# Waits in another order, epsilon on VectorE, a shorter normalise on GpSimd, and a new order of all pieces in a hybrid attention kernel

## The reference

```
x = x + window_attention(layernorm(x))      # 16 heads of 8, 2 key/value heads, windows of 32, keys 64 wide
x = x + butterfly_ffn(layernorm(x))         # 128 -> 512, gelu, 512 -> 128
x = x + linear_attention(layernorm(x))      # phi(x) = elu(x) + 1, phi(q) (phi(k)^T v) / (phi(q) sum phi(k) + 1e-6)
x = x + butterfly_ffn(layernorm(x))         # the same weights again
layernorm(x) = (x - mean) / sqrt(var + 1e-5)
```

## Time and profile before

| | us |
|---|---|
| median of 3 runs | 561.26 (560.38 to 562.34) |
| profiled execution, span from first to last instruction | 560.6 |
| TensorE busy | 525.0 |
| GpSimd busy | 450.9 |
| VectorE busy | 441.2 |
| ScalarE busy | 358.7 |
| instructions | 14708, of them 5060 matmuls |
| bytes moved | 38.88 MB, mean 69 GB/s |

### The profile page before, as it was taken

The page is one execution under the profiler, slowest core; times in us unless marked ns, Lnnn a source line. Parts: engine busy times, 40 slices in busy tenths (PEclk is TensorE's granted clock), DMA queues, the critical chain, the costliest instruction groups (busy, mean ns, idle before and its releaser), DMA issues. The chain is left out here.

```text
span 560.6 us, 14708 instructions
## 1 busy us (share of the span) xinstructions
PE 525.0 (94%) x5060; PEld 345.8 (62%) x5060; DVE 441.2 (79%) x1272; ACT 358.7 (64%) x578; POOL 450.9 (80%) x646
## 2 busy tenths in 40 slices
PE   5786998979999999999999999999999999999795
PEld 3442554546766666666667676666666667777563
DVE  5778789897888989898988898888989797663341
ACT  2543376567687767676777768686767777664532
POOL 6665689899898999999898989899999797955420
PEclk9789799989999999999999999999999999999899
DMA  9533232322223232232313231323232222100001
GB/s 310 170 76 81 63 83 54 81 74 56 54 58 80 62 76 66 68 78 48 102 45 87 63 87 44 84 60 77 61 76 50 59 66 58 39 1 20 1 20 37
DMA packets 49546, 38.88 MB, mean 69 GB/s; under 512 B 12352, under 2 KB 38976, under 8 KB 49472
## 3 DMA queue, kind: packets, MB, share of 16 engines
q1 hardware_dynamic: 47024, 33.73, 23.9%
q10 hardware_dynamic: 2448, 4.22, 2.1%
HBM read 15.64 MB, written 5.51 MB: 38 GB/s over the span
## 5 line engine op out<-in xcount | busy, mean ns | idle before, releaser
L501 POOL TENSOR_TENSOR probs_t<-probs_t,first 128x1024 f32<-128x1024 f32 x64 | 151.3, 2367 | 11.5 <-DMA probs_t<-probs_t 11.5
L645 PEld LDWEIGHTS ring<-w,early 128*128 128x128 f32 x1024 | 119.0, 192 | 9.6 <-issue 7.0
L982 ACT ACTIVATE early<-ring,b 128x512 f32<-128x512 f32 x128 | 87.2, 684 | 54.7 <-PE ring L633 53.1
L645 PE MATMUL ring<-w,early 128*128 128x128 f32 x1024 | 120.0, 275 | 0.8 <-ACT early L982 0.8
L972 ACT ACT_TABLE_LOAD x58 | 74.4, 1283 | 10.7 <-issue 9.7
L601 PE MATMUL ps_s<-kx,q_t 64*32 64x512 f32 x960 | 65.9, 606 | 3.4 <-DVE merged L1268 2.7
L633 PE MATMUL ring<-xT_G,w1b 128*128 128x512 f32 x128 | 67.1, 612 | 0.7 <-ACT xT_G L960 0.7
L991 ACT ACTIVATE probs_t<-merged_t 128x1024 f32<-128x1024 f32 x64 | 65.3, 1044 | 3.8 <-DVE merged_t L1275 3.7
L633 PE MATMUL ring<-xT_F,w1b 128*128 128x512 f32 x128 | 59.9, 611 | 0.4 <-ACT xT_F L960 0.4
L1255 DVE COPY_PREDICATED ps_s<-first,ps_s 128x512 f32<-128x512 uint32 x64 | 43.6, 681 | 9.2 <-PE ps_s L601 9.0
L1282 DVE STREAM_TRANSPOSE ps_o<-ps_o 128x512 f32<-128x512 f32 x64 | 46.2, 722 | 1.6 <-PE ps_o L618 0.3
(11 more groups left out here) (124 smaller groups left out, 1023.9 us busy)
## 6 DMA issues: line engine op xcount, KB each, us to landing
probs_t<-probs_t SPq DMA_DIRECT2D x256, 64.0 KB, 2.0
kx<-kv_rows SPq DMA_DIRECT2D x120, 40.0 KB, 2.2
x_P<-in_x SPq DMA_DIRECT2D x16, 256.0 KB, 3.2
out_x<-x_G SPq DMA_DIRECT2D x16, 256.0 KB, 2.4
vx_t<-kv_rows SPq DMA_DIRECT2D x128, 8.0 KB
up_s<-in_up_m ACTq DMA_DIRECT2D x7, 256.0 KB, 8.4
down_s<-in_down_m ACTq DMA_DIRECT2D x7, 256.0 KB, 8.4
kv_rows<-kv_t SPq DMA_DIRECT2D x16, 80.0 KB, 2.8
```

The costliest lines, as they stand in the source:

```text
L501: nc.gpsimd.tensor_tensor(parts, parts, keep.rearrange("p (a t) -> p a t", a=1).to_broadcast([P, PAIR * HEADS, WIN]), ALU.mult).then_inc(p ...
L645: last = nc.tensor.matmul(bank(name)[:, P * j:P * (j + 1)], hid[s][:, c, P * j:P * (j + 1)], w2[:, c], start=(c == 0), stop=(c == CH - 1))
L982: nc.scalar.activation(hid[s][:, c], bank(name)[:], ACT.Gelu, bias=b1[:, c:c + 1]).then_inc(drained[BANK[name]].sem, 1)
```

## The change

Four things change together.

1. **Waits.** In most pieces the wait that is expected to be met last stands first, and waits on the same semaphore are joined (`Count.both`). `COVERED` is drawn up anew; `scores` and `weighted_values` wait in every quarter that is not covered.
2. **Layernorm.** `moments` is split into `moments` (bn_stats), `moments_joined` (bn_aggr) and `variances_raised`, which adds epsilon on VectorE. GpSimd's `normalise` has five instructions: the power, and four `xn` = (x - mean) x rstd. VectorE's own `xn` is a piece, `normalise`.
3. **Pieces.** `head_outputs` is split into `heads_turned`, `sums_inverted`, `heads_divided`, and `linear_normalised` into `linear_sums`, `linear_sums_inverted`, `linear_divided`, so that other pieces can stand between them.
4. **Order.** All tables and all `turn` functions are new. The first two groups and the last three are placed piece by piece; in the full turns between, the order on TensorE stays close to the old one, with `W.proj` at the start of the next turn.

```diff
             def normalise(g, s):
-                pool.wait_ge(vec.sem, vec.after(g, f"{s}.mv"))
-                pool.wait_ge(pool_step.sem, pool_step.after(g - 1, f"{s}.nmr"))
-                nc.gpsimd.tensor_scalar(rv[s][:], mv[s][:, :, 1], LN_EPS, None, ALU.add).then_inc(pool_step.sem, 1)
-                nc.gpsimd.tensor_scalar(nm[s][:], mv[s][:, :, 0], -1.0, None, ALU.mult).then_inc(pool_step.sem, 1)
-                nc.gpsimd.tensor_tensor(rstd[s][:], rv[s][:], half[:], ALU.pow).then_inc(pool_step.sem, 1)
-                nc.gpsimd.tensor_tensor(nmr[s][:], nm[s][:], rstd[s][:], ALU.mult).then_inc(pool_step.sem, 1)
+                rooted_variance(g, s)      # waits for rv, then the power
+                pool.wait_ge(rooted.sem, rooted.after(g, f"{s}.rstd"))
                 pool.wait_ge(product.sem, product.after(g - 1, TURNED[s]))
                 for j in range(TILES):
-                    last = nc.gpsimd.tensor_scalar(xn[s][:, j], x_of(g, s)[:, j], rstd[s][:, j:j + 1],
-                                                   nmr[s][:, j:j + 1], ALU.mult, ALU.add)
+                    last = nc.gpsimd.tensor_scalar(xn[s][:, j], x_of(g, s)[:, j], mv[s][:, j, 0:1],
+                                                   rstd[s][:, j:j + 1], ALU.subtract, ALU.mult)
...
+            def variances_raised(g, s):
+                dve.wait_ge(vec.sem, vec.after(g, f"{s}.mv"))
+                nc.vector.tensor_scalar(rv[s][:], mv[s][:, :, 1], LN_EPS, None, ALU.add).then_inc(vec.sem, 1)
...
             def residual(g, s, name, base):
+                dve.wait_ge(product.sem, product.after(g, name))
                 if s == "G":
+                    dve.wait_ge(biased.sem, biased.after(g, f"{base}.xb"))
                     dve.wait_ge(y_out.sem, y_out.after(g - 1, "G.y"))
                 else:
+                    dve.wait_ge(biased.sem, biased.both((g, f"{base}.xb"), (g - 1, f"{s}.xb")))
                     dve.wait_ge(normed.sem, normed.after(g - 1, f"{s}.xn"))
-                    dve.wait_ge(biased.sem, biased.after(g - 1, f"{s}.xb"))
-                dve.wait_ge(biased.sem, biased.after(g, f"{base}.xb"))
-                dve.wait_ge(product.sem, product.after(g, name))
...
-                if s != "G":
-                    dve.wait_ge(own.sem, own.after(g, name))
```

More of the change, by code:

```diff
@@ L145, in after, with both @@
         return max(self.value(group, name) for name in names)
+    def both(self, *events):
+        return max(self.value(group, name) for group, name in events)
     def value(self, group, name):
@@ new lines, in turn @@
+                for g in due(t, 1, 2, 13):
+                    spread_probs(g, 1)
+                if t == 13:
+                    load_x(15)
+                if t == 6:
+                    store_y(0)
+                for g in due(t, 1, 14):
+                    spread_probs(g, 0)
+                for g in due(t, 1, 0, 12):
+                    spread_probs(g, 2)
+                if t == 2:
+                    spread_probs(1, 1)
+                for g in due(t, -1, 2, 12):
+                    store_keys(g)
@@ new lines, in turn @@
+                for g in due(t, 6, 2):
+                    store_y(g)
+                if t == 16:
+                    spread_values(15)
+                if t == 15:
+                    spread_keys(15)
+                if t == 14:
+                    store_keys(15)
+                for g in due(t, -2, 2, 14):
+                    load_x(g)
+                for g in due(t, 1, 1, 12):
+                    spread_probs(g, 3)
+                if t == 12:
+                    store_keys(13)
+                for g in due(t, 1, 14):
+                    spread_probs(g, 1)
@@ new lines, in turn @@
+                if t == 31:
+                    probs_parted(1, 1)
+                    add_bias(0, "W", bffn_s, "W.proj", "F.down")
+                for g in due(t, 30, 2, 12):
+                    probs_parted(g, 3)
+                for g in due(t, 0, 0, 1):
+                    add_bias(g, "P", bo_s, None, "W.proj")
+                if t == 1:
+                    normalise(1, "P")
+                    ffn_bias()
+                    up_diagonals()
+                    probs_parted(0, 0)
+                for g in due(t, 33, 0, 12):
+                    normalise(g, "L")
@@ new lines, in turn @@
+                if t == 44:
+                    probs_parted(14, 2)
+                if t == 42:
+                    normalise(15, "P")
+                for g in due(t, 30, 0, 1):
+                    probs_parted(g, 3)
+                for g in due(t, 32, 0, 12):
+                    add_bias(g, "F", bproj_s, "F.down", "L.proj")
+                if t == 44:
+                    probs_parted(14, 3)
+                for g in due(t, 31, 1, 12):
+                    add_bias(g, "W", bffn_s, "W.proj", "F.down")
@@ new lines, in turn @@
+                for g in due(t, 74, 14):
+                    add_bias(g, "L", bffn_s, "L.proj", "G.down")
+                if t == 88:
+                    rooted_variance(15, "L")
+                for g in due(t, 29, 14):
+                    probs_parted(g, 1)
+                if t == 44:
+                    normalise(13, "F")
+                    add_bias(14, "P", bo_s, None, "W.proj")
+                for g in due(t, 29, 2, 12):
+                    probs_parted(g, 1)
+                if t == 33:
+                    add_bias(0, "L", bffn_s, "L.proj", "G.down")
@@ L548, in turn @@
-                for g in due(t, 3, 2, 15):
-                    probs_parted(g, 1)
-                for g in due(t, 4, 0, 1):
-                    normalise(g, "W")
+                if t == 44:
+                    probs_parted(15, 2)
+                if t == 43:
+                    add_bias(13, "W", bffn_s, "W.proj", "F.down")
             for t in range(TURNS):
@@ new lines, in turn @@
+                if t == 2:
+                    scores_transposed(1, 3)
+                    values_out(1)
+                for g in due(t, 4, 2, 13):
+                    residual(g, "L", "L.proj", "F")
+                for g in due(t, 4, 2, 12):
+                    moments(g, "L")
+                if t == 16:
+                    merge_halves(15, 3)
+                for g in due(t, 2, 1, 13):
+                    residual(g, "W", "W.proj", "P")
+                    moments(g, "W")
+                if t == 14:
+                    attention_kv_out(15)
@@ new lines, in turn @@
+                if t == 14:
+                    heads_turned(13, 0)
+                for g in due(t, 2, 14):
+                    moments(g, "W")
+                    moments_joined(g, "W")
+                for g in due(t, 0, 2, 12):
+                    scores_transposed(g, 0)
+                for g in due(t, 0, 2, 13):
+                    merge_halves(g, 1)
+                if t == 4:
+                    residual(0, "L", "L.proj", "F")
+                if t == 3:
+                    variances_raised(1, "W")
@@ new lines, in turn @@
+                if t == 3:
+                    phi_q_made(0)
+                for g in due(t, 63, 14):
+                    residual(g, "G", "G.down", "L")
+                for g in due(t, 1, 14):
+                    sums_inverted(g, 0)
+                if t == 16:
+                    phi_q_made(13)
+                    subtract_max(15, 3)
+                    phi_k_made(13, 1)
+                    heads_divided(15, 0)
+                for g in due(t, 3, 0, 12):
+                    phi_k_made(g, 1)
@@ new lines, in turn @@
+                if t == 15:
+                    scores_transposed(15, 0)
+                    heads_divided(14, 0)
+                if t == 14:
+                    merge_halves(14, 2)
+                if t == 12:
+                    moments(14, "P")
+                if t == 6:
+                    residual(1, "G", "G.down", "L")
+                for g in due(t, 0, 2, 12):
+                    merge_halves(g, 2)
+                if t == 12:
+                    moments_joined(14, "P")
+                for g in due(t, 3, 2, 12):
+                    phi_q_made(g)
@@ new lines, in turn @@
+                if t == 3:
+                    linear_sums(0, 0)
+                    linear_sums_inverted(0, 0)
+                if t == 1:
+                    up_bias_out()
+                    residual(0, "W", "W.proj", "P")
+                    moments(0, "W")
+                    moments_joined(0, "W")
+                    variances_raised(0, "W")
+                for g in due(t, 1, 2, 12):
+                    heads_turned(g, 2)
+                    sums_inverted(g, 2)
+                if t == 13:
+                    scores_transposed(13, 2)
```

1484 lines of the change are left out of this document (933 added, 551 removed), and 112 rows, old and new, of tables (COVERED, PARTED, PROBS, PRODUCTS).

## The result

| us | before | after |
|---|---|---|
| median | 561.25 (560.38 to 562.34) | 584.88 (583.19 to 586.41) |
| profiled span | 560.6 | 584.5 |
| TensorE, GpSimd, VectorE, ScalarE busy | 525.0, 450.9, 441.2, 358.7 | 523.9, 493.6, 460.0, 353.6 |

The ratio is 1.0417 (95% interval 1.0386 to 1.0448): 23.6 us slower, where 13.5 us faster was forecast.

What follows compares the result with a forecast made beforehand. TensorE, busy 94% of the span, was taken to bound the kernel. Head -7.1 and end -6.4, full turns nothing, gave -13.5 on 560.6: 547.1, and a median of 547.8 us, range 541 to 557.

Steps and rivals of the forecast that it cites:

- the price of xn: In GpSimd's normalise: four xn stay at 1.75 us, 0.87 x 4 = 3.5 us a turn saved, GpSimd 23.5 of 30.24.
- The slack on GpSimd: In the window from 146.10 to 508: GpSimd busy 27.0 us per turn of 30.24, so covered by TensorE.
- The raises: Four epsilon additions of 128x4 a turn on VectorE: 0.15 us each, +0.6 a turn, at most +2.9.
- hidden, price 0: VectorE in full turns: between 24.9 and 28.6 of 30.24 us with the raises, so they add nothing to the time.
- The full turns: Middle of the kernel: same matmuls and changes of tiling, turns stay 30.24 us if nothing new is late; gain nothing.
- The head: -7.1: Start to first full turns: x_W of group 0 at 58 us (-4.5), then -2.6 more; bounds 0 and -15.
- half-clock pieces: In the head's x_W(0) term, -4.5: W.S0(2) and P.kv(3) now stand behind W.proj(0), and TensorE pieces at half clock with them.
- The end: -6.4: Last groups: stall at L.oT(14) goes, 1.0 lost at L.xT(15), G.xT(15) at 540.8 instead of 547.27; bounds -4 and -7.5.
- The order on VectorE: Full turns: 12 places instead of 20 where a step directly follows the one it needs, 8 x 0.17 = 1.4 us back.
- The rival that the order is worth nothing there: On VectorE the 1.4 us a turn fail; full turns hide it, three turns of the head do not: 552 us; chance 0.06.
- A new wait in every full turn: Rival, chance 0.12: x_W late on VectorE makes TensorE wait before F.xT; 1.2 us in 11 turns eats the gain, 1.7 gives 567.

Runs made afterwards that it cites:

- The form alone: Kernel before with only GpSimd's four xn changed to subtract, multiply, nm and nmr still made but unused: 625.0 us, ratio 1.1166.
- the whole normalise alone: Kernel before with the new normalise (epsilon on VectorE, power and four xn by subtract, multiply on GpSimd), old order and waits: 582.96 us, ratio 1.0406.
- the same order with the old form: New kernel with xn again by multiply, add, GpSimd making nm and nmr, epsilon still on VectorE: 557.63 us, ratio 0.9955.
- the forms by themselves: No kernel: pairs of tensor_scalar operations on 128x128 with nothing else busy; on GpSimd multiply, add took 0.45 us and subtract, multiply 0.80.
- five steps: New kernel, VectorE making rv and the negated mean in one 128x8 instruction, GpSimd the power and four xn by add, multiply: 555.63 us, ratio 0.9917.
- eight steps: New kernel with the whole old normalise on GpSimd, epsilon too, leaving only the new order, split pieces and waits: 559.57 us, ratio 1.0023.
- the raise alone: Kernel before with only epsilon moved to VectorE inside moments, GpSimd keeping its other seven steps: 560.75 us, ratio 1.0009.
- seven steps: Normalise with epsilon on GpSimd, nmr gone, xn by add, multiply: new kernel 551.64 us, ratio 0.9867; kernel before 561.76 us, ratio 1.0015.

## Why the prediction was wrong

**The failed step: the price of xn.** "Only pow (1.04) and a step of 0.1 stand ahead of xn. That is 0.87 x 4 = 3.5 us less, 23.5 of 30.24" kept the 1.75 us of four xn through a change of their operations, from multiply, add to subtract, multiply. No row of before showed that pair on GpSimd, and it was not bounded as an unknown. It takes 3.13 (50.1 us in 16 groups). 244 instructions by 0.347 us are 84.7 more, the steps saved 64 by 0.67, 42.9: +41.8, measured +42.7. So GpSimd went from 450.9 us to 493.6 instead of 408, and set the length of the full turns, for which the prediction had the price 0: 31.6 us each in place of 30.24. The form alone, the whole normalise alone, the same order with the old form, and the forms by themselves show this step from four sides.

**The slack on GpSimd.** "Per turn the same window gives GpSimd 27.0 us" is a mean over 146.10 to 508, where the last groups already run out. A full turn, from 206.60 to 236.80, has 27.8. Of the 2.4 idle us of such a turn, 1.7 are gaps between GpSimd's own steps; waits for other engines make up 0.7. The form alone shows the same slack: 16 xn by 0.347 add 5.55 us to a turn, and the turn grew by 4.85, from 30.24 to 35.09. And "3.5 us less" took a road for busy time: 0.87 a normalise counts the gaps, while busy time fell by 2.7 a group with five steps.

**The raises: nearest row, wrong kind.** "I take 0.15, nearer in kind and size" took a norm read from PSUM as the like of a raise between SBUF tiles. What decided was where the operands lie and what GpSimd is running, not the size. The bound from above, 2.9 us a turn, was near: 64 raises took 40.4 us, 2.5 a group. The old order does not test "hidden, price 0": its raises stay at 0.17 to 0.21 us, and nothing is to be hidden (1.0009). In the new one, turns 11 to 15 lose some 4 to 5 us to them: 152.2, 152.3 and 153.1 us with all raises on VectorE, 147.6 and 148.6 without those of P and L. The 151.2 with eight steps is no counter-example: no raise is on VectorE there, but TensorE waits for the long normalise.

**The full turns.** The order itself keeps 30.15 to 30.25 us a turn, as forecast. That groups 13 to 15 leave the pattern of the full turns in turns 11 to 15 was not weighed: P.xT(13) and P.xT(14) stand earlier there, and with a long normalise TensorE waits 2.1 us at each.

**The head: -7.1.** The first scores and x_W(0) came within 0.3 us; x of group 1 had landed by 8.83 and not at 10.0, but the first keys kept the scores where they were forecast. The four kernels with the new order and xn by add, multiply reach PV0(4) at 135.2 to 138.6, on the mean 137.4; the three old ones with multiply, add or add, multiply at 142.9 to 146.1, 144.3. Less the 0.9 us of pieces that changed sides, the gain is 6.0. The size is near the forecast, the mechanism is not. Windows from the start to PV0(4), of the kernel before, the same with the raise alone, and the new one with seven steps:

```profile
0.00:146.10 146.10, 121.78 (x1148) 70.32 (x1148) 117.53 (x317) 75.14 (x124) 112.49 (x156) 0.93 0.36 101
```
```profile
0.00:142.90 142.90, 116.86 (x1148) 66.94 (x1148) 122.41 (x331) 75.05 (x124) 108.67 (x142) 0.98 0.37 103
```
```profile
0.00:138.30 138.30, 113.71 (x1140) 65.44 (x1140) 114.33 (x316) 73.94 (x123) 107.88 (x140) 0.99 0.39 108
```

TensorE idles 24.3, 26.0 and 24.5 us ahead of PV0(4) in the three old kernels, and 22.5 to 24.6, on the mean 23.4, in the four new ones: 1.5 us of shorter waits. The rest is busy time, 119.4 against 114.0 on the mean, at a granted clock of 0.93, 0.98 and 0.95 against 0.99 to 1.00. The forecast had named "half-clock pieces" in one of its terms and put the rest on shorter waits.

**The clock over the whole kernel.** It moves the time of the kernel before from one execution to the next. In the 68 timed executions of it that count beside the experiments its mean is 0.978 to 0.997, and the times are 554.68 to 562.91 us; the four with 0.994 or more took 554.68 to 556.68. The new order with five to eight steps, xn not by subtract, multiply, had 0.99 or more in each that counts. So its gain is in part a higher clock: seven steps in the new order took 551.64 us, 7.6 below the median of before beside it, but only 3 to 5 below the three executions of before beside it at 0.994 to 0.997. With eight steps, 559.57 us, the new order is slower than before at a like clock, for all its own clock of 0.99 to 1.00. Why the new order keeps the clock up was not tried.

**The end: -6.4.** No wait at L.oT(14), 0.50 at L.xT(15) (forecast 1.0), and 9.7 us behind G.xT(15) (forecast 9.8), in the kernel after. From PV0(15) on the same four kernels take 81.5 us on the mean, the three old ones 86.2: 4.7, with 1.3 us more of pieces done in it, so 6.0. Here waits did go: TensorE idles 7.8 us on the mean in place of 11.3.

**The order on VectorE.** 1.4 us a turn was forecast from putting strangers between dependent steps. With the same instructions VectorE is busy 424.3 us in the new order against 441.2: 1.06 a group. Of the 16.9 us, 11.9 are instructions that overlap their predecessor more, the rest are shorter ones. The rival that the order is worth nothing there fell, and these numbers do not agree with the rule of the Trainium skill that the prediction set beside it (VectorE: DVE Perf Modes, The DRAIN you can't avoid).

**The rivals.** "A new wait in every full turn" had the right side and the right kind, 11 waits of L.xT for xn_F, 11.4 us in all. Its cause, a late x_W, and its bar, the slack on GpSimd, were wrong: that slack was 0.7 us a turn.

Added up, order and split are worth 0.9867 / 1.0015 = 0.985, 8 us, with a normalise of seven steps, the higher clock included, and nothing measurable with eight (1.0023). That difference is shown by the waits for xn (13.1 against 4.7 us) and not taken apart further. The change of the waits' sequence was not tried by itself.

## What to carry to other kernels

When an edit rewrites an instruction, its old duration is no longer a row for it, even if shape and engine stay: price the new pair of operations and the new places of the operands as unknown, bound them by the engine's other groups, and look what the upper bound would do to the engine's share of a turn. An engine's slack is not one minus its busy share: here GpSimd was busy 92% of a full turn and had 0.7 us of 30.24 to give. Count its own gaps as work, and take the share from one full turn, not from a stretch in which the work runs out. A small tensor_scalar or tensor_tensor on VectorE between SBUF tiles can last as long as what GpSimd is doing at that moment, so put it where GpSimd idles, or on GpSimd. And when an order is compared with another, compare the granted clock of several executions too, before the gain is put down to shorter waits.

## What the runs showed of the hardware

- GpSimd, tensor_scalar on 128x128 fp32 with scalars per partition: 0.45 us for multiply, add; add, multiply; multiply, multiply; 0.80 for the three pairs with a subtract and for add, add; 0.605 with one operation alone, so two cheap operations cost less than one.
- VectorE beside a busy GpSimd: 1.9 us for 128x4 between SBUF tiles, 0.15 into PSUM, 0.16 for a reciprocal; three elements a partition instead of four change nothing: 1.91 in five of six, 0.40 in the first, which started late in a multiply (1.66 on the mean). In the kernels one raise took 3.20 us, through two instructions of GpSimd, one 3.68 (old form, new order), and one of 128x8 4.84, each through three. Where GpSimd idled, the raise took 0.17.
- The granted clock differs between executions of one kernel: its mean over the span of the kernel before is 0.978 to 0.997, with 562.91 us at 0.979 and 554.96 at 0.997.
- GpSimd leaves gaps of up to 0.18 us between its own instructions: 1.73 us in a turn of 41.
